# Experts' down projection in five split products, one plain chunk in gate/up, and a new order of the experts' steps

## The reference

```python
gx = xp[buf_tok]                                   # 64 experts x 128 rows x 512
gu = jnp.einsum('ech,ehi->eci', gx, gate_up_proj)  # 512 -> 384
g, u = jnp.split(gu, 2, axis=-1)
hid = jax.nn.silu(g) * u                           # 192 columns
eo = jnp.einsum('eci,eih->ech', hid, down_proj) * buf_w[..., None]
routed = jnp.zeros((T + 1, h), x.dtype).at[buf_tok.reshape(-1)].add(eo.reshape(-1, h))[:T]
shared = jax.nn.silu(xf @ shared_gate_w.T) * (xf @ shared_up_w.T) @ shared_down_w.T
```

## Time and profile before

| | us |
|---|---|
| median of 3 runs | 957.72 |
| lowest and highest | 955.71, 958.39 |
| span of the profiled execution (first to last instruction) | 945.2 |

### The profile page before, as it was taken

The page is one execution under the profiler, slowest core; times in us unless marked ns, Lnnn a source line. Parts: engine busy times, 40 slices in busy tenths (PEclk is TensorE's granted clock), DMA queues, the critical chain, the costliest instruction groups (busy, mean ns, idle before and its releaser), DMA issues. The chain is left out here.

```text
span 945.2 us, 15175 instructions
## 1 busy us (share of the span) xinstructions
PE 918.1 (97%) x4626; PEld 727.5 (77%) x4626; DVE 683.3 (72%) x1250; ACT 499.5 (53%) x1015; POOL 460.9 (49%) x540
## 2 busy tenths in 40 slices
PE   9999999999999999998999999999999999999996
PEld 7788888888888888776787777777777677767875
DVE  7996878879797877987766666665655565636776
ACT  5543434344443535453456665666555566545775
POOL 2002456665656656677135445554545544433564
PEclk9999999999999999999999999999999999999998
DMA  7244735434342516275569999999999999969972
GB/s 209 89 155 121 176 90 158 117 108 132 125 127 75 177 59 204 79 268 173 174 196 302 308 322 322 321 316 318 322 287 307 305 305 303 322 113 392 382 259 111
DMA packets 114190, 203.91 MB, mean 216 GB/s; under 512 B 18496, under 2 KB 56384, under 8 KB 113088
## 3 DMA queue, kind: packets, MB, share of 16 engines
q1 hardware_dynamic: 93584, 159.87, 51.6%
q0 software_dynamic: 19520, 35.75, 16.7%
q10 hardware_dynamic: 1008, 7.34, 2.2%
HBM read 143.03 MB, written 59.88 MB: 215 GB/s over the span
## 5 line engine op out<-in xcount | busy, mean ns | idle before, releaser
L1535 POOL DMA_INDIRECT slot_table<-tokens,slot_of x162 | 181.0, 1118 | 86.7 <-issue 50.3
L1577 POOL DMA_INDIRECT acc_rows<-eo,table_sb x64 | 110.6, 1729 | 172.5 <-ACT eo L888 127.2
L1632 PE MATMUL bank<-x_hi,wqkv_hi 128*128 128x512 f32 x384 | 152.1, 396 | 0.3 <-DVE wqkv_lo L972 0.3
L1632 PE MATMUL bank<-x_hi,wqkv_lo 128*128 128x512 f32 x384 | 150.2, 391 | 0.0
L1632 PE MATMUL bank<-x_lo,wqkv_hi 128*128 128x512 f32 x384 | 150.2, 391 | 0.0
L1404 DVE TENSOR_TENSOR wgu_lo<-wgu,wgu_hi 128x1536 fp32r<-128x1536 f32 x64 | 112.4, 1758 | 48.0 <-ACT wgu_hi L882 48.0
L1632 PE MATMUL bank<-wdn,hid_et 96*128 96x512 f32 x256 | 122.8, 602 | 8.2 <-ACT hid_et L924 8.2
L882 ACT CAST wgu_hi<-wgu 128x1536 fp32r<-128x1536 f32 x64 | 94.5, 1477 | 5.8 <-DMA wgu<-w_gu 5.4
L1566 POOL DMA_INDIRECT xg<-x_rows,table_sb x64 | 74.3, 1162 | 41.3 <-DVE table_sb L1133 22.0
L1632 PE MATMUL bank<-wgu_hi,xgt_hi 128*128 128x384 f32 x256 | 91.4, 357 | 0.0
L1632 PE MATMUL bank<-wgu_hi,xgt_lo 128*128 128x384 f32 x256 | 85.9, 335 | 0.0
(11 more groups left out here) (183 smaller groups left out, 2146.0 us busy)
## 6 DMA issues: line engine op xcount, KB each, us to landing
wgu<-w_gu SPq DMA_DIRECT2D x64, 768.0 KB, 8.5
wdn<-w_down SPq DMA_DIRECT2D x64, 384.0 KB, 8.5
xres<-x SPq DMA_DIRECT2D x32, 256.0 KB, 2.9
x_turned<-x1t SPq DMA_DIRECT2D x32, 256.0 KB
x_rows<-x SPq DMA_DIRECT2D x32, 256.0 KB, 3.0
acc_rows<-x SPq DMA_DIRECT2D x32, 256.0 KB, 3.1
fin<-acc_rows SPq DMA_DIRECT2D x8, 1024.0 KB, 12.1
odd<-acc_rows SPq DMA_DIRECT2D x8, 1024.0 KB, 13.9
```

What stands on the lines that cost most here:

```text
L1535: pool.indirect_dma_start(table_dram, bass.IndirectOffsetOnAxis(slot_of[:, i, k:k + 1], 0), tokens[:, i:i + 1], None, bounds_check=SLOTS - ...
L1577: pool.indirect_dma_start(acc_dram[e % 2], bass.IndirectOffsetOnAxis(table_sb[:, e:e + 1], 0), eo[eo_slot[e]][:, :], None, bounds_check=T ...
L1632: mm = pe.matmul(out_ap, a, b, start=first and i == 0, stop=final and i == len(products) - 1)
```

## The change

1. `down` is five split products. The 192 inner rows are 128 and 64. The first 128 take three products with `wdn_hi` and `wdn_lo`. The other 64 are packed: `wdn_mix` holds, on its two halves of 64 partitions, the high and the low part of the 64 rows (for the first 256 columns high on top, for the others low on top), and the hidden columns 128 to 191 stand twice in `hid_e`, so that two products, with `het_hi` and `het_lo`, give all parts. `w_down` is laid out as 128 x 768 rather than 96 x 1024, in four buffers rather than three; the fourth is loaded a little later before the loop.
2. Gate/up: the last of four chunks is one plain fp32 product (`xgt_full`), issued first; the other three stay split (`KS = 3`).
3. ScalarE computes silu itself (`silu_e`, and `silu_s` in the units of all blocks but the first), which takes one more load of a function table; VectorE's part of silu goes.
4. New order. TensorE: gate/up of e, units, `down(e - 1)`, `turn_rows(e + 2)`, hidden rows of e. The rows are turned two experts ahead. ScalarE and VectorE follow, with `split_down_of` for the new parts of w_down, and `turned_low` for `het_lo`.
5. Some semaphores are joined into one.

The diff, cut to what the prediction speaks of:

```diff
-    IH = I // 2
+    IB = I - P
+    DH = D // 2
+    DN = D + DH
+    KS = KC - 1
...
-    NG, ND, NXG, AHEAD = 4, 3, 6, 4
+    NG, ND, NXG, AHEAD = 4, 4, 6, 4
...
+    wdn_buf = [both.place(f"wdn{i}", [P, DN]) for i in range(2)]
...
-            for e in range(2, ND):
+            load_down(2)
+            sp.wait_ge(heads_mm, NB)
+            for e in range(3, ND):
...
-                act.copy(xgt_hi[e % 2][:, :, :], xg_ps[:, :].rearrange("p (k s) -> p k s", k=KC)).then_inc(xgt_hi_done, 1)
+                turned = xg_ps[:, :].rearrange("p (k s) -> p k s", k=KC)
+                act.copy(xgt_full[e % 2][:, :, :], turned[:, KS:KC, :])
+                act.copy(xgt_hi[e % 2][:, :, :], turned[:, 0:KS, :]).then_inc(xgt_hi_done, 1)
 
             def split_expert(e):
                 act.wait_ge(gu_in[e % NG], 16 * (e // NG + 1))
                 if e >= 2:
                     act.wait_ge(gu_mm, e - 1)
-                act.copy(wgu_hi[e % 2][:, :, :], wgu_buf[e % NG][:, :, :]).then_inc(wgu_hi_done, 1)
+                act.copy(wgu_hi[e % 2][:, :, :], wgu_buf[e % NG][:, 0:KS, :]).then_inc(wgu_hi_done, 1)
+
+            def split_down_of(e):
+                act.wait_ge(dn_in[e % ND], 16 * (e // ND + 1))
+                if e >= 2:
+                    act.wait_ge(eo_mm, e - 1)
+                w, mix = wdn_buf[e % ND], wdn_mix[e % 2]
+                act.copy(wdn_hi[e % 2][:, :], w[:, 0:D])
+                act.copy(mix[0:IB, 0:DH], w[0:IB, D:DN])
+                act.copy(mix[IB:P, DH:D], w[IB:P, D:DN]).then_inc(wdn_hi_done, 1)
...
             for e in range(NE):
                 act.wait_ge(gu_mm, e + 1)
                 if e:
-                    act.wait_ge(silu_e_done, e)
-                act.activation(tanh_e[:, :], gu_ps[e % 2][:, 0:I], ACT.Tanh, scale=0.5).then_inc(tanh_e_done, 1)
-                if e + 1 < NE:
-                    split_rows(e + 1)
+                    act.wait_ge(hid_e_done, e)
+                act.activation(silu_e[:, :], gu_ps[e % 2][:, 0:I], ACT.Silu).then_inc(silu_e_done, 1)
                 if e + 2 < NE:
                     split_expert(e + 2)
+                for _ in range(fills_of[e]):
+                    unit()
                 if e:
                     scale_rows(e - 1)
-                for _ in range(fills_of[e]):
-                    unit()
                 act.wait_ge(ht_mm, e + 1)
                 if e >= 2:
                     act.wait_ge(eo_mm, e - 1)
-                act.copy(hid_et[e % 2][:, :, :], ht_ps[0:IH, 0:2 * P].rearrange("p (h s) -> p h s", h=2)).then_inc(hid_et_done, 1)
+                act.copy(het_hi[e % 2][:, :, :], ht_ps[:, 0:2 * P].rearrange("p (h s) -> p h s", h=2)).then_inc(het_hi_done, 1)
+                if e + 2 < NE:
+                    split_rows(e + 2)
+                if e + 1 < NE:
+                    split_down_of(e + 1)
             scale_rows(NE - 1)
...
+            def split_down_of(e):
+                dve.wait_ge(wdn_hi_done, e + 1)
+                w, mix = wdn_buf[e % ND], wdn_mix[e % 2]
+                dve.tensor_tensor(wdn_lo[e % ND][:, :], w[:, 0:D], wdn_hi[e % 2][:, :].bitcast(F32), ALU.subtract)
+                dve.tensor_tensor(mix[IB:P, 0:DH], w[0:IB, D:DN], mix[0:IB, 0:DH].bitcast(F32), ALU.subtract)
+                dve.tensor_tensor(mix[0:IB, DH:D], w[IB:P, D:DN], mix[IB:P, DH:D].bitcast(F32), ALU.subtract).then_inc(wdn_lo_done, 1)
+
+            def turned_low(e):
+                dve.wait_ge(het_hi_done, e + 1)
+                if e >= 2:
+                    dve.wait_ge(eo_mm, e - 1)
+                dve.tensor_tensor(het_lo[e % 2][:, :, :], ht_ps[:, 0:2 * P].rearrange("p (h s) -> p h s", h=2),
+                                  het_hi[e % 2][:, :, :].bitcast(F32), ALU.subtract).then_inc(het_lo_done, 1)
...
             for e in range(NE):
                 ps = gu_ps[e % 2]
-                dve.wait_ge(tanh_e_done, e + 1)
-                if e:
-                    dve.wait_ge(hid_e_done, e)
-                dve.scalar_tensor_tensor(out=silu_e[:, :], in0=tanh_e[:, :], scalar=1.0, in1=ps[:, 0:I],
-                                         op0=ALU.add, op1=ALU.mult).then_inc(silu_e_done, 1)
                 dve.wait_ge(silu_e_done, e + 1)
                 if e >= 2:
                     dve.wait_ge(ht_mm, e - 1)
-                dve.scalar_tensor_tensor(out=hid_e[e % 2][:, :], in0=silu_e[:, :], scalar=0.5, in1=ps[:, I:GU],
-                                         op0=ALU.mult, op1=ALU.mult).then_inc(hid_e_done, 1)
-                if e + 1 < NE:
-                    split_rows(e + 1)
+                dve.tensor_tensor(hid_e[e % 2][:, 0:I], silu_e[:, :], ps[:, I:GU], ALU.mult)
+                dve.tensor_tensor(hid_e[e % 2][:, I:2 * P], silu_e[:, P:I], ps[:, I + P:GU], ALU.mult).then_inc(hid_e_done, 1)
+                split_down_of(e)
+                if not fills_of[e]:
+                    turned_low(e)
                 if e + 2 < NE:
                     split_expert(e + 2)
-                for _ in range(fills_of[e]):
-                    unit()
+                if fills_of[e]:
+                    for _ in range(fills_of[e]):
+                        unit()
+                    turned_low(e)
+                if e + 2 < NE:
+                    split_rows(e + 2)
...
             def down(e):
-                pe.wait_ge(hid_et_done, e + 1)
-                pe.wait_ge(dn_in[e % ND], 16 * (e // ND + 1))
+                pe.wait_ge(het_lo_done, e + 1)
+                pe.wait_ge(wdn_lo_done, e + 1)
                 if e:
                     pe.wait_ge(eo_done, e)
-                chain(eo_ps[:, :], [(hid_et[e % 2][:, k, :], wdn_buf[e % ND][:, k, :]) for k in range(2)]).then_inc(eo_mm, 1)
+                products = three(het_hi[e % 2][:, 0, :], het_lo[e % 2][:, 0, :], wdn_hi[e % 2][:, :], wdn_lo[e % ND][:, :])
+                products += [(part[e % 2][:, 1, :], wdn_mix[e % 2][:, :]) for part in (het_hi, het_lo)]
+                chain(eo_ps[:, :], products).then_inc(eo_mm, 1)
...
             for e in range(NE):
                 pe.wait_ge(xgt_lo_done, e + 1)
-                pe.wait_ge(wgu_lo_done, e + 1)
                 if e >= 2:
                     pe.wait_ge(hid_e_done, e - 1)
-                products = []
-                for k in range(KC):
+                pe.wait_ge(wgu_lo_done, e + 1)
+                products = [(xgt_full[e % 2][:, k - KS, :], wgu_buf[e % NG][:, k, :]) for k in range(KS, KC)]
+                for k in range(KS):
                     products += three(xgt_hi[e % 2][:, k, :], xgt_lo[e % 2][:, k, :], wgu_hi[e % 2][:, k, :], wgu_lo[e % NG][:, k, :])
                 chain(gu_ps[e % 2][:, 0:GU], products).then_inc(gu_mm, 1)
-                if e + 1 < NE:
-                    turn_rows(e + 1)
+                for _ in range(fills_of[e]):
+                    unit()
                 if e:
                     down(e - 1)
-                for _ in range(fills_of[e]):
-                    unit()
+                if e + 2 < NE:
+                    turn_rows(e + 2)
                 pe.wait_ge(hid_e_done, e + 1)
                 if e:
-                    pe.wait_ge(hid_et_done, e)
-                for k in range(2):
-                    mm = pe.transpose(ht_ps[0:IH, k * P:(k + 1) * P], hid_e[e % 2][:, k * IH:(k + 1) * IH], ident[:, :])
+                    pe.wait_ge(het_lo_done, e)
+                for h in range(2):
+                    mm = pe.transpose(ht_ps[:, h * P:(h + 1) * P], hid_e[e % 2][:, h * P:(h + 1) * P], ident[:, :])
                 mm.then_inc(ht_mm, 1)
...
-    down = down.reshape(experts, 2, inner, D).transpose(0, 2, 1, 3)
+    rest = down[:, P:].reshape(experts, -1, 2, half).transpose(0, 2, 1, 3).reshape(experts, P, half)
+    down = np.concatenate([down[:, :P], rest], axis=2)
```

More of the change, by code:

```diff
@@ L89, in build @@
     wgu_buf = [both.place(f"wgu{i}", [P, KC, GU]) for i in range(2)]
-    wdn_buf = [both.place(f"wdn{i}", [IH, 2, D]) for i in range(2)]
+    wdn_at = [both.at + 4 * i * DN for i in range(2)]
+    wdn_buf = [both.place(f"wdn{i}", [P, DN]) for i in range(2)]
     att = Map(nc, both.at, end)
@@ L198, in build @@
     wgu_buf += [late.place(f"wgu{i}", [P, KC, GU]) for i in range(2, NG)]
-    wgu_lo = [Map(nc, at, at + 4 * KC * GU).place(f"wgu_lo{i}", [P, KC, GU], F32R) for i, at in enumerate(wgu_at)]
-    wdn_buf += [late.place(f"wdn{i}", [IH, 2, D]) for i in range(2, ND)]
-    assert late.at <= projected_end + 8 * 4 * BT
+    wgu_lo = [Map(nc, at, at + 4 * KC * GU).place(f"wgu_lo{i}", [P, KS, GU], F32R) for i, at in enumerate(wgu_at)]
+    wdn_at += [late.at + 4 * i * DN for i in range(ND - 2)]
+    wdn_buf += [late.place(f"wdn{i}", [P, DN]) for i in range(2, ND)]
+    wdn_lo = [Map(nc, at, at + 4 * D).place(f"wdn_lo{i}", [P, D], F32R) for i, at in enumerate(wdn_at)]
+    assert late.at >= projected_end + 8 * 4 * BT
     shared_rows = [late.place(f"shared_rows{b}", [P, NJ, D]) for b in range(EARLY - SET)]
@@ L206, in build @@
     xg = [late.place(f"xg{i}", [P, D + E]) for i in range(NXG - 2)]
```

(22 more changed lines are left out.)

54 lines of the change are left out of this document (31 added, 23 removed).

## The result

| | us |
|---|---|
| before, median of 4 runs | 958.06 (955.71 to 962.74) |
| changed kernel, median of 4 runs | 946.41 (945.86 to 948.09) |
| ratio | 0.9887, 95% interval 0.9838 to 0.9936 |
| span of the changed kernel's profiled execution | 944.2 |

The change is worth 11.6 us, 1.1%. Forecast were 948.2 us. I read the changed kernel's trace in the same order as that of before.

A forecast was written before the change was run, and what follows sets the result against it. It took TensorE (346 of the loop's 357 us) and the gapless DMA engines as both near their limit. 2.3 us before 510 us plus 7.2 after, 9.5 off 957.7, gave 948.2 us; own range 941 to 955.5, overall 930 to 966.

The forecast's parts named there:

- The TensorE term: Experts' loop: down -0.59 us, gate/up +0.126, net -0.465 us an expert, -29.3 us over 63, pace 3.99 us.
- upper price: Gate/up's plain product up to 0.86 us, turning hidden rows up to +0.08; with these TensorE gains only 11 us in all.
- A cut on TensorE is worth only what the DMA engines can follow: Experts' loop: after 510 us, 100.5 MB at 314 GB/s limit the gain to 7.2 us; 9.5 us in all.
- The first rival: DMA follows: 307 GB/s is only what TensorE asked for; loop falls by 29.3 us, total 928.4 us; chance 0.15.
- Both stay under the pace of 3.99, so I cost the splitting of w_down at nothing: Experts' loop: ScalarE needs 3.5 us and VectorE 3.6 us an expert, so the splitting hides beside TensorE.
- each 0.1 us of excess costs 4.2 us: If TensorE no longer covered the splitting, each 0.1 us over the pace would count on 42 experts without a unit.
- So one expert in three has ScalarE waiting about 0.5 us at L902: ScalarE's gate/up cast: the load's window shrinks from 9.4 to 8.0 us, while a load lands after 8.5 us.
- The gather two experts ahead: Rows turned two experts ahead: gather has three steps, about 15 us, against 9.5 us for landing.
- The loads of w_down keep their 384 KB ... in four buffers rather than three: Down weights' loads: same size, as 128 rows rather than 96, one buffer more; no time was put on it.
- The third rival: Additions, two at a time, make it slower if landing grows past 11.3 us; 966.4 us at 11.6; chance 0.18.
- The second rival: DMA already at its ceiling: rate stays 307 GB/s, only the ramp is gained, 955.4 us; chance 0.17.
- The offset of 12.5 us: Profiled span of before, 945.2 us, lies 12.5 us under its median of 957.7; taken as constant.

The follow-up runs named there:

- e3: Kernel before, with w_down loaded for the first three experts only and later experts reusing the buffers: 944.15 us, loop 346.1 us.
- e12: Changed kernel with ScalarE's wait before scaling rows moved to the addition of e-3 (same kernel as e10): median 922.38 us, ratio 0.9746, loop 330.2 us.
- e5: Changed kernel, unaltered, traced a second time: 935.08 us, loop 344.5 us.
- e6: Changed kernel without ScalarE's two casts of the packed part of w_down from the third expert on: 933.32 us, loop 343.1 us.
- e7: Changed kernel without VectorE's subtractions for w_down (one 32-column piece stays; high part used for low): 925.17 us, loop 335.7 us.
- e10: Changed kernel with ScalarE, before scaling rows, waiting for the addition of e-3 itself; single execution: 920.63 us, loop 330.9 us.
- e8: Changed kernel with three buffers for w_down rather than four: 946.94 us, loop 356.5 us.
- e1: Kernel before, unchanged, traced a second time: 954.77 us, loop 356.9 us.
- e4: Kernel before with the last chunk of the experts' gate/up products left out, nine products rather than twelve: 948.74 us, loop 350.7 us.
- e9: Kernel before with four buffers for w_down rather than three: 949.64 us, loop 360.4 us.
- e11: Changed kernel with e10's wait, het_hi ahead of the scaled rows on ScalarE, wgu_lo and units ahead of het_lo on VectorE: median 934.2 us, ratio 0.9881, loop 344.4 us.

## Why the prediction was right, and where it was wrong

**The TensorE term** held: down 1.16 for 1.13, step 4.02 for 3.99. The plain 384-column product went with its columns, as taken. The one upper price that came true is turning the hidden rows, 0.22 for 0.14. The 3.99 also held 0.09 us that twelve split products took beyond 12 x 0.173 (2.17 for 2.08); the parts measured here add up to 4.02 without it. That two such differences cancel is luck. e3 shows the floor of 346.1 us to the tenth.

**"A cut on TensorE is worth only what the DMA engines can follow"** was right in its size and wrong in its reason. Forecast: the loop's bytes at a middle rate of 314 GB/s, 9.5 us gained. Measured: 320 GB/s after the ramp, 12.2 to 13.8 us gained in the loop. The rate was a result. The forecast also called 340 GB/s more than the best 8 us of before, which its trace contradicts (356 over 538 to 546 us, 354 over 812 to 820). A DMA share at or above 1 was read as engines with no room. But the share is 1.04 at 307 GB/s in before and 1.02 at 333 in e12, with the same transfers. It counts the time that packets take, and that can be had at either rate. The first rival was right in that (the rate is what is asked for), and wrong in who asks: for it TensorE would have had to be the only other bound. By the Trainium skill (DMA: Bandwidth & Descriptors, Specifications) the limit is about 358 GB/s. The traces go beyond it: 372 GB/s over the 52 us from 848, and 376 over 544 to 552 us in the changed kernel's loop. Over the whole of a loop's 300 us no run came near it (333 in e12).

So that 948.2 lies within 2 us of 946.4 is partly luck. The sum took away from TensorE's term what DMA bandwidth was thought to forbid. By the runs it goes like this: 316.8 us for TensorE alone, 10.4 more for a pace of 4.16 rather than 3.99 (327.2, an estimate), 3.0 more in e12, and 14.3 more in e5 for the wait on the wrong addition.

**"Both stay under the pace of 3.99, so I cost the splitting of w_down at nothing"** is the step that failed. ScalarE takes 4.16 us a step for 3.5 forecast, VectorE 4.15 for 3.6, so neither had slack. Of ScalarE's 0.63 us, 0.34 are the two casts of 64x256: 0.43 each from start to start (621.46, 621.89, 622.32), where 256 x 0.871 + 39 ns gave 0.26. Of these 0.17 us, 0.05 are a longer duration (0.42 and 0.41, where 256 x 0.871 + 139 ns is 0.36). The rest is the 0.1 us that the forecast took off every instruction as hidden beside the next: nothing is hidden here. The first cast ends at 621.46 + 0.42 = 621.88 and the next starts at 621.89. het_hi, as many columns but read from PSUM, ends at 620.53 and the next starts at 620.41, so it takes 0.25. silu_e behind the casts takes 0.36 for a duration of 0.33, and 0.23 in e6, where the casts are gone: 0.13 more. VectorE shows the same: its three splits of w_down take 0.70, 0.43 and 0.50 us (the next instruction, het_lo, starts at 620.56) for durations of 0.69, 0.42 and 0.42, 0.4 us over their forecast. What takes the overlap away (64 partitions rather than 128, or two instructions that write halves of one tile) no run separates.

The Trainium skill (Perfetto Trace Analysis, Optimizing Scalar/DVE Operations) gives ScalarE about 93 ns of overhead an instruction on SBUF and 51 on PSUM. The trace agrees with the direction: the cast from SBUF lasts 0.42 us and het_hi from PSUM 0.37. That is not enough for the 0.18 us between their start-to-start times.

I had the rule "each 0.1 us of excess costs 4.2 us" ready. It would have made 0.17 us into 7 us. No run tests it as such: taking work off VectorE gave 7.4 to 8.8 us (e7), taking it off ScalarE alone nothing that shows (e6).

**"So one expert in three has ScalarE waiting about 0.5 us at L902"** didn't happen: no wait for the gate/up load, as landings fell to 7.5 us (e5). The window is also longer than the 8.0 forecast: two steps of 4.16 and silu_e's 0.36 make 8.7. In e10, with a faster loop, it is there (6.8 us in 6 waits) and costs little. At TensorE, het_lo was waited for 10.3 us, where I had some 20 for it and L902 together. The gather two experts ahead was waited for next to nowhere (0.4 us) in the changed kernel, as forecast, and for 4.6 us in e12.

**"The loads of w_down keep their 384 KB ... in four buffers rather than three"** missed a moved need. I gave the fourth buffer no price; 12 us hang on it (e8). It wasn't spare but paid for the splitting, which wants the weights about one and a half steps earlier. The rule was followed for gate/up and the gather and not for this load.

**The third rival**, additions two at a time, was wrong on landing (8.9 us, not over 11), and named the right resource: the additions held up the loop, through ScalarE's queue and not POOL's. The 35.4 us in the earlier trace rows stood in plain sight; the parity of the experts where they fall was not looked at. **The second rival** fell: the rate did rise.

**The offset of 12.5 us** was not time around the span. A timed execution takes 2 to 3 us more than its span (946.57 and 944.2 for the change, 954.77 and 952.7 in e1). In these traces the start of the loop goes with the chip and not with the kernel: 487.3 to 487.9 us in e1 to e4, 480.2 to 482.5 in e5 to e8 and e12, 479.2 to 480.3 in e9 to e11, the first and the third group with kernels of both orders in them. The trace of before, with 480.6 and a span of 945.2, looks like those of the second and third chip, where before takes 945 to 947 us, and not like runs of 957.7; on which chip it was taken isn't known. As only a difference was formed, the forecast survived it. In the changed kernel's trace the loop starts at 493.5, of which 6.4 us are a stop told below, in e5 at 481.2, so this isn't the change's.

What stays open: how the wait for e - 3 would do in the old order, whether e12 with less on ScalarE and VectorE would come nearer to TensorE's 316.8 us, how much of each wait's cost is TensorE's clock, and why POOL's issue of an addition takes longer in the new kernel (mean 2.20 us in the loop, 1.73 before, 1.72 in e11). Without VectorE's work on w_down it stays at 2.23 (e7), so it isn't that.

## What to carry to other kernels

When work is moved off a full engine, write out the whole step of the engines that take it, start to start, and don't take off a hidden end for instructions that no trace has shown next to each other. An engine filled to the pace can't absorb a wait. Before a resource is called a ceiling, look at which waits end on it and at which iterations they fall: a wait for one item too new looks like a slow DMA, and the same line can wait for one too old elsewhere and protect nothing. For each operand that a new step reads, count again from its load to its first reader, buffer by buffer.
